# Normalising x on ScalarE, with an offset from Pool, instead of on VectorE

## The reference

```python
def layer_norm(x, scale, bias):
    m = jnp.mean(x, axis=-1, keepdims=True)
    v = jnp.mean(jnp.square(x - m), axis=-1, keepdims=True)
    return (x - m) * jax.lax.rsqrt(v + EPS) * scale + bias
...
tgt = tgt + _self_attn(layer_norm(tgt), mask, ...)     # layer 0
tgt = tgt + (memory @ Wg.T + bg)
x = tgt + (relu(layer_norm(tgt) @ W1.T + b1) @ W2.T + b2)
...
x = mha(y1, y1, causal=True) + x                       # layer 1, y1 = layer_norm(x)
y = mha(layer_norm(x), ctx, causal=False) + x
out = y + relu(layer_norm(y) @ W1 + b1) @ W2 + b2
```

## Time and profile before

| | |
|---|---|
| time, median of 3 runs | 1516.67 us (1515.88 to 1516.74) |
| the profiled execution | 1518.18 us, span 1516.4 us |
| TensorE busy | 1411.4 us |
| VectorE busy | 1163.5 us |
| ScalarE busy | 1040.2 us |
| Pool busy | 833.7 us |

### The profile page before, as it was taken

The page is one execution under the profiler, slowest core; times in us unless marked ns, Lnnn a source line. Parts: engine busy times, 40 slices in busy tenths (PEclk is TensorE's granted clock), DMA queues, the critical chain, the costliest instruction groups (busy, mean ns, idle before and its releaser), DMA issues.

```text
span 1516.4 us, 39426 instructions
## 1 busy us (share of the span) xinstructions
PE 1411.4 (93%) x13620; PEld 1164.5 (77%) x13620; DVE 1163.5 (77%) x3860; ACT 1040.2 (69%) x2104; POOL 833.7 (55%) x1138
## 2 busy tenths in 40 slices
PE   6889999999999999998888888889999999999987
PEld 5679989988998988876666676657777777777757
DVE  3888888888888888778788778777777776777653
ACT  4777777777777776666666666676666677676663
POOL 4455555555555565655555545545665656665532
PEclk8999999999999999999999999999999999999999
DMA  6454443344434434444554555563344333444200
GB/s 179 146 153 128 126 112 112 113 116 121 127 113 112 121 115 121 143 126 131 162 161 130 154 158 144 154 170 107 106 127 136 100 113 105 114 130 127 77 29 15
DMA packets 161589, 187.09 MB, mean 123 GB/s; under 512 B 15984, under 2 KB 136176, under 8 KB 161392
## 3 DMA queue, kind: packets, MB, share of 16 engines
q1 hardware_dynamic: 161104, 183.78, 42.4%
q10 hardware_dynamic: 288, 0.79, 0.2%
HBM read 125.78 MB, written 58.72 MB: 122 GB/s over the span
## 4 chain that ended last, share of the span: by engine, by line
PE 70%; DVE 12%; issue 7%; ACT 7%; POOL 3%; DMA 1%; SPq 1%; ACTq 0%; DVEq 0%; POOLq 0%
PE d_ps L514 28%; PE o_ps L664 9%; PE d_ps L817 9%; PE s_ps L586 7%; PE t_ps L600 7%; PE t_ps L634 4%; DVE prob L1049 3%; PE m_ps L521 2%; ACT q_stack L879 2%; DVE o_q L1137 1%; ACT prob_t L871 1%; ACT h_f L979 1%; DVE top L1034 1%; ACT xt_hi L888 1%; PE m_ps L681 1%
## 5 line engine op out<-in xcount | busy, mean ns | idle before, releaser
L871 ACT ACTIVATE prob_t<-t_ps 128x384 f32<-128x384 f32 (+1 forms) x512 | 276.1, 547 | 258.3 <-PE t_ps L634 150.4
L586 PE MATMUL s_ps<-k_stack,q_stack 96*128 96x256 bf16 (+1 forms) x1536 | 284.8, 267 | 36.0 <-DVE top L1049 23.5
L862 ACT ACTIVATE prob<-prob,neg_max 128x256 f32<-128x256 f32 x512 | 230.9, 505 | 64.8 <-DVE neg_max L1049 61.8
L1291 POOL TENSOR_TENSOR h_lo<-h_f,h_hi 128x512 fp32r<-128x512 f32 x124 | 159.4, 1285 | 112.9 <-DVE h_hi L1181 102.8
L1049 DVE CUSTOM_DVE_ANT_0 prob<-s_ps,bias_sb 128x256 f32<-128x256 f32 x512 | 194.5, 417 | 30.3 <-PE s_ps L586 28.2
L586 PEld LDWEIGHTS s_ps<-k_stack,q_stack 96*128 96x128 bf16 x1536 | 115.8, 98 | 127.8 <-issue 51.2
L1034 DVE TENSOR_REDUCE top<-s_ps 128x2 f32<-128x512 f32 x256 | 170.4, 681 | 49.4 <-PE s_ps L586 47.9
L634 PE MATMUL t_ps<-q_stack,k_stack 108*128 108x256 bf16 (+1 forms) x1024 | 201.6, 264 | 4.1 <-ACT q_stack L879 4.1
L1049 DVE CUSTOM_DVE_ANT_0 prob<-s_ps,causal 128x128 f32<-128x128 f32 (+1 forms) x512 | 156.9, 351 | 46.9 <-PE s_ps L586 46.1
L664 PE MATMUL o_ps<-prob_t,v_sb 128*17 128x256 f32 (+1 forms) x3072 | 192.0, 368 | 0.0
L600 PE MATMUL t_ps<-ident_sb,prob 128*128 128x128 f32 x1024 | 155.9, 274 | 1.3 <-DVE prob_t L1247 1.2
(11 more groups left out here) (155 smaller groups left out, 4012.5 us busy)
## 6 DMA issues: line engine op xcount, KB each, us to landing
parts<-q_part SPq DMA_DIRECT2D x96, 192.0 KB, 2.3
parts<-k_part SPq DMA_DIRECT2D x96, 192.0 KB, 2.3
q_stack<-parts SPq DMA_DIRECT2D x96, 192.0 KB, 3.3
k_stack<-parts SPq DMA_DIRECT2D x94, 192.0 KB, 3.3
q_stack<-parts SPq DMA_DIRECT2D x96, 128.0 KB, 3.1
k_stack<-parts SPq DMA_DIRECT2D x94, 128.0 KB, 3.2
ct_kept<-ct_hl SPq DMA_DIRECT2D x16, 512.0 KB, 3.4
x_in<-x_mid SPq DMA_DIRECT2D x32, 256.0 KB, 3.6
```

The source lines that it names most:

```text
L586: last = mm(s_ps[:, h % 2, q * S:q * S + n], q_stack[0:ROWS, t.par, head_of(t, h), q * P:(q + 1) * P], k_stack[0:ROWS, t.par, head_of(t, h ...
L862: last = nc.scalar.activation(prob[:, h % 4, q, :], prob[:, h % 4, q, :], ACT.Exp, bias=neg_max[:, h % 4, q:q + 1], scale=-1.0)
L871: nc.scalar.activation(prob_t[:, h % 8, 0:n], t_ps[:, h % 2, 0:n], ACT.Exp, scale=-1.0)\
L1291: g.tensor_tensor(dst, a, b, ALU.subtract).then_inc(done, 1)
```

## The change

ScalarE normalises x, as out = scale * x + offset, with scale = rstd and offset = -mean * rstd for each token. Pool makes the offset with two operations of 128x2 right behind the power: mean * rstd, then 0 minus that, each waiting for the one before. The two operations of 128x256 on VectorE go. It is on for all kinds of steps (`X_ON_ACT = (0, 1, 2)`). In ScalarE's order the new work stands in slot `LN_AT[2]`, behind the keyed exponential and the row maximum copy of that slot, ahead of the transposed copy and of pass 0's exponential of it. The two other switches are off (`X2_ON_ACT`, `H_ON_ACT` are empty), and `h_on_act` takes the place of `tail or end` with the same meaning.

```diff
+X_ON_ACT, X2_ON_ACT = (0, 1, 2), ()
...
+        offset, offset2 = sb("offset", [P, TT]), sb("offset2", [P, TT])
...
+        ln_off, ln2_off = ev("ln_off", 2), ev("ln2_off", 2, MLP)
...
@@ block.scalar
+                if h == st.ln_at[2] and has(st.nxt2) and st.x_on_act:
+                    act.wait_ge(ln_off.sem, ln_off.after(st.nxt2))
+                    for t in range(TT):
+                        x = x_in[:, st.nxt2.par, t, :]
+                        last = nc.scalar.activation(x, x, ACT.Identity, bias=offset[:, t:t + 1], scale=rstd[:, t:t + 1])
+                    last.then_inc(x_hat.sem, 1)
                 if h == st.xf_at + 1 and has(st.nxt2):
...
@@ block.vector
-                if h == st.ln_at[2] and has(st.nxt2):
+                if h == st.ln_at[2] and has(st.nxt2) and not st.x_on_act:
                     dve.wait_ge(ln_rstd.sem, ln_rstd.after(st.nxt2))
                     normalise(x_in[:, st.nxt2.par], x_in[:, st.nxt2.par], mv, rstd, x_hat)
...
@@ block.gpsimd
                     g.tensor_tensor(rstd[:, :], ve[:, :], minus_half[:, :], ALU.pow).then_inc(ln_rstd.sem, 1)
+                    pool.wait_ge(ln_rstd.sem, ln_rstd.after(st.nxt2))
+                    g.tensor_tensor(offset[:, :], mv[:, :, 0], rstd[:, :], ALU.mult).then_inc(ln_off.sem, 1)
+                    pool.wait_ge(ln_off.sem, 2 * ln_rstd.after(st.nxt2) - 1)
+                    g.tensor_tensor(offset[:, :], zeros[:, :, 0], offset[:, :], ALU.subtract).then_inc(ln_off.sem, 1)
```

More of the change, by code:

```diff
@@ L92 @@
 TAIL_AT = 0, (7, 8, 9, 10), 12, (12, 13, 14, 15)
+H_ON_ACT = ()
 O_AT = (13, 14, 13)
@@ L125, in __init__ @@
         self.norm_at = NORM_AT[self.kind]
+        self.x_on_act, self.x2_on_act = self.kind in X_ON_ACT, self.kind in X2_ON_ACT
         self.o_at = O_AT[self.prev.p] if self.prev else None
         self.tail, self.end = s == NTASK, s == NTASK + 1
+        self.h_on_act = self.tail or self.end or self.kind in H_ON_ACT
         if self.tail:
@@ L967, in slot @@
                     if n >= 2:
-                        if not (st.tail or st.end):
+                        if not st.h_on_act:
                             act.wait_ge(h_h.sem, h_h.after(st.old, n - 1))
                         act.wait_ge(h_l.sem, h_l.after(st.old, n - 1))
-                    for f in range(2 if st.tail or st.end else 0):
+                    for f in range(2 if st.h_on_act else 0):
                         c = C_B1 + FT * MLP.index(st.old.p) + 2 * n + f
@@ L974, in slot @@
                                                     ACT.Relu, bias=cols_sb[:, c:c + 1])
-                    if st.tail or st.end:
+                    if st.h_on_act:
                         last.then_inc(h_h.sem, 1)
@@ L1177, in slot @@
                     minus(h_lo[:, 2 * n:2 * n + 2, :], h_f[:, n % 2], h_hi[:, 2 * n:2 * n + 2, :], h_l.sem)
-                if h - 2 in st.w1_at and has(st.old, MLP) and not (st.tail or st.end):
+                if h - 2 in st.w1_at and has(st.old, MLP) and not st.h_on_act:
                     n = st.w1_at.index(h - 2)
@@ L1342, in slot @@
                     n = st.w1_at.index(h - 2)
-                    if st.tail:
+                    if st.h_on_act:
                         pool.wait_ge(h_done.sem, h_done.after(st.old, n + 1))
```

## The result

The kernel after takes 1521.19 us (median of 10 runs, 1518.77 to 1523.23) against 1516.70 for the kernel before: a ratio of 1.0026, with a 95% interval of 1.0017 to 1.0035. By the ratio it is slower by 3.9 us (by the two medians, 4.5) where 3.3 us less were forecast, and it lies above 1520.5, the upper end of the range. The profiled execution took 1523.23 us, its span 1521.4, 5.0 more than the span of before.

A forecast was written before the change was run, and what follows sets the result against it. TensorE was taken as the bound (93% busy), only pass 1 being shortenable through VectorE. Terms -6.6 + 0.9 + 2.3 + 0.1 = -3.3 us took 1516.67 to 1513.4 us; own range 1511 to 1516, overall range 1509.5 to 1520.5.

The forecast's parts named there:

- pass 0 and pass 2: Steps of these passes: no change, as TensorE has no idle time that the removed VectorE work could shorten.
- Pass 1, 14 x 0.47 = 6.6: Pass 1 form steps: o_f starts earlier, winning 0.47 us in each of 14 of the 16 steps, 6.6 us.
- the links: Pool's two new 128x2 operations: each link, with its semaphore, takes 0.28 us, 0.56 together.
- the collision: Pass 1: Pool's second operation falls on the o_n pair and slips between, costing VectorE about 0.05 us, Pool 0.1.
- Rivals 1: Pass 1: Pool waits for the whole o_n pair, a step wins 0.2 us at most; 1517.2 us, no change; chance 0.14.
- Rival 3: Pass 1: VectorE's length isn't the limit, waits re-form and only the costs stay; 1520.0 us, slower; chance 0.08.
- rival 4: Pass 1: the full 0.64 us is won in all 16 steps, 10.2 us; 1509.8 us; chance 0.10.
- Step 17, +0.9: First pass 2 form step (650 us): its transposes already wait for x_in, so it costs 0.9 us.
- Pass 2, nothing: Pass 2: x ready at 1210.90, transposes start at 1211.07, so free by 0.17 us; no gain either.
- Rival 2: Pool to ScalarE link: each Pool operation costs 0.25 us more, x is 0.5 later everywhere; 1524.7 us, slower; chance 0.08.
- The start, +2.3: Program start: normalising queues behind six DMA issues, first scores 4.6 us later, partly offset by a higher clock; +2.3 us.
- Step 32: Pass 1 step with the context load (976.6 us): wins nothing, as TensorE waits for a DMA issued no earlier.

The follow-up runs named there:

- e1: The kernel after with its new tiles offset and offset2 allocated last, so every other tile keeps its address of before: 1514.66 us, ratio 0.9984 to the kernel before.
- e3: The change in pass 1 alone, new tiles last, VectorE normalising elsewhere as before: 1511.50 us, ratio 0.9961 to the kernel before.
- e8: The change from step 0 on, new tiles last, with the normalisings ahead of step 0 left on VectorE: 1510.64 us, ratio 0.9958 to the kernel before.
- e11: e8 plus four unused tiles, ahead of ve, ot_hi, x2t_hi and h_hi: 1508.00 us, ratio 0.9943 to the kernel before.
- e2: The kernel before with one unused tile of 64 bytes ahead of ve: 1525.73 us, ratio 1.0057.
- e5: The kernel before with one unused tile of 64 bytes ahead of w_hi, so all tiles move, weights too: 1516.64 us, ratio 0.9998.
- e6: The kernel before with one unused tile of 128 bytes ahead of ve: 1520.01 us, ratio 1.0017.
- e7: The kernel before with one unused tile of 64 bytes ahead of h_hi: 1521.18 us, ratio 1.0031.
- e9: The kernel before with 670 TensorE products behind its end, other engines idle, operands at various shifts; ran once, its time of no interest.
- e10: The change everywhere but in pass 1, new tiles last: 1520.63 us, ratio 1.0030 to the kernel before.
- e12: The kernel before with the same four unused tiles as e11 and nothing else: 1515.31 us, ratio 0.9989.
- e4: The kernel before with two unused tiles of 64 bytes, ahead of ve and ahead of ot_hi: 1515.22 us, ratio 0.9985.

## Why the prediction was wrong

- **The term that was missing.** The sum had nothing for pass 0 and pass 2, "TensorE has no idle time" there. That reading was right, and at the layout of before the two passes do stay put (e1: 35.46 and 32.27 in the mean). The failed step is a silent one: that TensorE's own work costs the same. In a pass where TensorE is the bound, each of its products counts, and of the 198 groups of MLP products (five or more of a kind in a row) in steps 2 to 43, none was above 118.6 ns in the mean before and 183 were after. The whole of it, the kernel after against e1, is worth 6.4 us. None of the four rivals had it.
- **Without it the forecast holds.** The change at the layout of before has 0.9984, 1514.2 us on the 1516.7 of the forecast, inside its own range of 1511 to 1516. Part of that is luck: the start cost 1.6 more than forecast (3.9), and terms of a few tenths went the other way. In e1's trace steps 18 to 34 brought 6.4 (6.6 forecast), steps 14 to 18 cost 0.6 (0.9), and pass 2 and the end are 0.5 below the trace of before.
- **Pass 1, 14 x 0.47 = 6.6.** Right. The timelines of the step in the kernel after, answering:

```profile
874.34 0.69 POOL L1381 TENSOR_TENSOR rstd<-ve,minus_half 128x2 f32<-128x2 f32 x1 [0.52 <-DVE ve L1077]
875.11 0.20 POOL L1383 TENSOR_TENSOR offset<-mv,rstd 128x2 f32<-128x2 f32 x1
875.20 0.76 DVE L1136 TENSOR_TENSOR o_n<-o_q,rden 128x256 f32<-128x256 f32 x2
875.38 0.29 POOL L1385 TENSOR_TENSOR offset<-zeros,offset 128x2 f32<-128x2 f32 x1
875.71 1.09 ACT L1006 ACTIVATE x_in<-x_in,offset,rstd 128x256 f32<-128x256 f32 x2 [0.31 <-POOL offset L1385]
876.00 0.71 DVE L1154 STREAM_TRANSPOSE o_f<-o_n 128x512 f32<-128x512 f32 x1
876.86 0.65 PE L527 MATMUL m_ps<-ident_sb,x_in 128*128 128x128 f32 x4
879.00 0.33 PE L592 MATMUL s_ps<-k_stack,q_stack 96*128 96x128 bf16 x2
```

  The pair takes 1.09 us (1.1 forecast), the links 0.27 (0.28). Pool's second operation does slip in beside the o_n pair: it takes 0.29 instead of 0.20, and the pair stays at 0.76, so the collision cost Pool 0.1 and VectorE nothing. o_f starts 0.80 behind o_n instead of 1.32, a gain of 0.52 where 0.51 was the best case; the transposes are 1.83 behind the power's end (1.76), and the scores that had waited 0.58 come without a wait, 0.52 earlier against the power. Rivals 1 (Pool waits for the pair) and 3 (nothing but costs) fall with e3, and rival 4 (0.64 us in all 16 steps) with the 0.52 measured.
- **Step 17, +0.9.** Right: +0.99. The timelines of Pool and PE, answering; 0.24 of idle time became 1.05:

```profile
655.04 0.69 POOL L1381 TENSOR_TENSOR rstd<-ve,minus_half 128x2 f32<-128x2 f32 x1
657.46 0.66 PE L527 MATMUL m_ps<-ident_sb,x_in 128*128 128x128 f32 x4 [1.05 <-ACT x_in L1006]
```

- **Pass 2, nothing.** Right as to the wait: the transposes start 2.17 behind the power's end and wait for nothing. Rival 2 (a dear link, 1524.7) falls with it. Its sum was off as well: x 0.65 us late against 0.88 of idle time leaves some 0.2 a step in pass 1 by the working of rival 1, not 0.06. Rival 3 (nothing but costs, 1520.0) came nearest to the time, by luck: the gain of pass 1 is there, and the cost that made up for it is in none of its terms.

```profile
1210.71 0.69 POOL L1381 TENSOR_TENSOR rstd<-ve,minus_half 128x2 f32<-128x2 f32 x1
1211.98 1.09 ACT L1006 ACTIVATE x_in<-x_in,offset,rstd 128x256 f32<-128x256 f32 x2 [2.24 <-POOL offset L1385]
1213.57 0.60 PE L527 MATMUL m_ps<-ident_sb,x_in 128*128 128x128 f32 x4
```

- **The start, +2.3.** The mechanism was right (queue of six DMAs, first scores at 34.4 to 36.0 for a forecast 35.2, clock kept up behind them), the size was not: 3.9 by the timed runs, as a gain of 2.0 was credited against a low clock that two of eleven traces had. The +2.8 of the table agrees with the forecast because it is taken against the same trace.
- **Step 32.** The load of the context was said to win nothing. TensorE waited 2.17 us for it after, where it had waited 0.54:

```profile
977.93 0.51 PE L520 MATMUL d_ps<-ct_hl,w_hi 128*128 128x256 f32 x2 [2.17 <-DMA ct_hl<-ct_kept]
```

  In the other traces with the faster pass 1 this wait is 1.6 (e1), 1.8 (e3), 0.7 (e8) and 1.5 (e11), without it 0.3 to 1.3 in seven (e2, e5, e6, e7, e9, e10, e12) and 2.1 in e4. The two ranges overlap, and kernels with the same pass 1 differ by more than a microsecond, so whether the faster pass 1 lengthens this wait is not shown.

## What to carry to other kernels

A tile added in the middle moves every tile behind it, and where TensorE is the bound that can cost more than the change brings: allocate new tiles last, or leave the distance between weights and data as it was, and compare the pace of the products before any wait is compared. An engine that is busy longer with the same instructions is not waiting for anybody, so no chain of waits will show it. Moving work to another engine also moves it behind what that engine issues, and a price of the start that is read from one execution needs a second one.

## What the runs showed that was not expected

A product of TensorE (128x128 stationary, 256 columns moving) had three paces at the full clock: 113, 118 and 120 ns. A distance of a multiple of 128 bytes between the two operands gave 119 to 120 on an idle core, and mostly so in the kernels (the ot products 118.4 in pass 0, and no group of any kind under 117.7); an odd multiple of 64 gave 113 or 118, in groups, and moving h by 64 bytes changed the pace of the ot products in pass 0, whose operands had stayed (118 to 113). On the idle core the pattern repeated after 256 bytes, in the full kernels it did not. The transposes through ident_sb (109 ns) and the products of k_stack with q_stack (256 columns, 114 to 115 in the median) and of prob_t with v_sb had the same pace in all kernels.
